# Layers 3 and 4 of a small four-layer model: integer weights and x in two rounded pieces, and a new order on ScalarE

## The reference, cut to what matters

```python
def _dequant(w_int, dtype):            # w_int: int32 from -127 to 127
    return w_int.astype(dtype) * jnp.asarray(1.0 / 127.0, dtype)
gate = jnp.einsum('bsd,hd->bsh', x, wg)      # 128 features -> 384 hidden
up = jnp.einsum('bsd,hd->bsh', x, wu)
h = jax.nn.silu(gate) * up
return jnp.einsum('bsh,dh->bsd', h, wd)

xn = _layernorm(x, axis=-1)            # layer 3: local attention over 5 neighbours
x = x + _L2_attn_ref(xn, ...) + _L2_ffn_ref(xn, w_gate, w_up, w_down)
xn = _layernorm(x, axis=-1)            # layer 4: linear attention with normed heads
x = x + _L3_attn_ref(xn, ...) + _L3_ffn_ref(xn, w_gate, w_up, w_down)
```

## Time and profile before

| | us |
|---|---|
| median of 3 runs (707.17, 710.59, 707.20) | 707.2 |
| the profiled execution's own time | 706.8 |
| its span, first to last instruction | 704.9 |
| TensorE matmul busy in the span | 604.3 (86%) |
| TensorE weight loads | 402.8 (57%) |
| VectorE | 459.6 (65%) |
| ScalarE | 390.2 (55%) |
| GpSimd | 370.7 (53%) |
| mean granted TensorE clock | 0.95 of full |

### The profile page before, as it was taken

How to read it: one execution, slowest core, us unless ns; L and a number is a source line. 1 busy time by engine, 2 the same in 40 slices (tenths; PEclk the granted TensorE clock), 3 DMA queues, 4 the chain that set the end, 5 groups by cost and what they waited for, 6 DMA issues and landing times. The chain is left out here.

```text
span 704.9 us, 9323 instructions
## 1 busy us (share of the span) xinstructions
PE 604.3 (86%) x3100; PEld 402.8 (57%) x3100; DVE 459.6 (65%) x824; ACT 390.2 (55%) x802; POOL 370.7 (53%) x291
## 2 busy tenths in 40 slices
PE   5999888799999988886978698589997888898877
PEld 2433444445454445564667478487887767565546
DVE  6797899999898969754545975133333556445643
ACT  3589899779799744554699352122211237333340
POOL 0688698899899945776101728509014620112220
PEclk9999799999999999997999889689998999999999
DMA  4043333346566401002400114106121100000002
GB/s 117 4 119 57 74 92 103 92 119 128 130 126 127 104 14 54 0 1 76 130 1 2 31 16 139 42 4 167 38 53 37 28 4 1 1 1 0 1 0 60
DMA packets 45817, 40.40 MB, mean 57 GB/s; under 512 B 12183, under 2 KB 32585, under 8 KB 45770
## 3 DMA queue, kind: packets, MB, share of 16 engines
q1 hardware_dynamic: 44746, 37.71, 22.5%
q0 software_dynamic: 1024, 2.10, 1.0%
HBM read 33.70 MB, written 6.09 MB: 56 GB/s over the span
## 5 line engine op out<-in xcount | busy, mean ns | idle before, releaser
L408 PE MATMUL bank<-l0s_ring,all_ident 128*128 128x512 f32 x256 | 120.2, 605 | 4.8 <-POOL l0s_ring L664 4.8
L795 DVE TENSOR_TENSOR_SCAN l0s_ring<-l_XM,l0s_carry,bank 128x512 f32<-128x512 f32 x62 | 74.8, 1257 | 6.3 <-PE bank L391 6.3
L408 PEld LDWEIGHTS bank<-l0s_ring,all_ident 128*128 128x128 f32 x256 | 46.4, 194 | 52.5 <-issue 42.9
L664 POOL TENSOR_TENSOR l0s_ring<-l0s_ring,all_XF 128x1024 f32<-128x1024 f32 x31 | 65.1, 2116 | 10.3 <-DVE l0s_ring L795 9.8
L664 POOL TENSOR_TENSOR l0s_ring<-l0s_ring,l0s_c_rest 128x1024 f32<-128x1024 f32 x32 | 65.4, 2058 | 9.2 <-DVE l0s_ring L795 3.3
L551 ACT ACTIVATE all_XNT<-l_wraw,l_wins 128x256 f32<-128x256 f32 x156 | 66.1, 496 | 0.3 <-PE bank L391 0.2
L391 PEld LDWEIGHTS bank<-all_ident,all_XNT 128*128 128x128 f32 x312 | 36.3, 142 | 34.7 <-issue 26.3
L391 PE MATMUL bank<-all_ident,all_XNT 128*128 128x128 f32 x312 | 42.8, 277 | 10.5 <-DVE l0s_ring L795 7.9
L530 ACT ACTIVATE l_XM<-l_DT,l_negA 128x512 f32<-128x512 f32 x78 | 51.4, 710 | 0.0
L795 DVE TENSOR_TENSOR_SCAN l0s_ring<-bank,l0s_carry,l0s_ring 128x512 f32<-128x512 f32 x34 | 41.5, 1261 | 1.8 <-POOL l0s_ring L654 1.8
L654 POOL TENSOR_TENSOR l0s_ring<-l_DTU,l0s_b_all 128x1024 f32<-128x1024 f32 x20 | 41.0, 2052 | 0.0
(11 more groups left out here) (423 smaller groups left out, 1546.0 us busy)
## 6 DMA issues: line engine op xcount, KB each, us to landing
l0s_c_rest<-bc_rows SPq DMA_DIRECT2D x16, 512.0 KB, 5.4
all_XF<-bc_rows SPq DMA_DIRECT2D x16, 512.0 KB, 5.3
l0s_b_all<-bc_rows SPq DMA_DIRECT2D x20, 256.0 KB, 6.3
l_wall<-in_L_ffn_W SPq DMA_DIRECT2D x14, 256.0 KB, 4.7
all_X<-in_L_attn_x SPq DMA_DIRECT2D x4, 256.0 KB, 3.7
gx<-l1m_TD SPq DMA_DIRECT2D x1, 1024.0 KB, 5.2
gy<-l1m_TD SPq DMA_DIRECT2D x1, 1024.0 KB, 8.6
out<-all_X SPq DMA_DIRECT2D x4, 256.0 KB, 2.3
```

What stands on the lines that cost most here:

```text
L408: last = nc.tensor.matmul(bank_y[j][:, :], S.ident[:, :], hc[n % CRING][:, j, :], start=False, stop=(n % DS == DS - 1))
L664: nc.gpsimd.tensor_tensor(hc[n % CRING][:, :, :], h[n % RING][:, :, :], wide(c_wide[p % HRING][:, n % 2, :]), ALU.mult).then_inc(hc_ready, 1)
L795: nc.vector.tensor_tensor_scan(h[n % RING][:, j, :], factor, added, before, ALU.mult, ALU.add).then_inc(h_ready, 1)
```

## The change

- S.ffn's gate and up weights are stored as F32R (float32r, a 4-byte format that TensorE reads rounded), and hold the integers themselves; the factor 1/127 is applied in silu (scale=QSCALE) and in hidden, which becomes scalar_tensor_tensor.
- x of a block is split in two pieces, xhi (rounded on writing, upper_part, on ScalarE) and xlo = x - xhi (lower_part, on GpSimd, for block 0 on VectorE). gate and up are then two f32r matmuls each, one for each piece, into the same bank.
- upper_part and lower_part have places in the orders of ScalarE, GpSimd and VectorE, and gate_up waits for both pieces.
- silu(3) comes before attend(4) of the local attention; in the loop the first silu of a block comes before heads_squares.
- The four matmuls against the identity in down(b) get is_transpose=True.
- Four weight tiles of layer 4 (wqkv3, bwide, wo3, bow) move into the space of E.w0 (expert 0's weights, used in the stage before).

In the diff, hunks stand in the order GpSimd, TensorE, ScalarE, VectorE. Not shown are lower_part(6) and lower_part(7), which stand behind scale(1) and scale(2) as the others do, and the up's matmuls, which change as the gate's.

```diff
+QSCALE = 1.0 / 127.0
-        ...activation(dst, ..., ACT.Copy, scale=1.0 / 127.0)
+        ...activation(dst, ..., ACT.Copy, scale=1.0 if n % 3 < 2 else QSCALE)
...
-                wqkv3 = ph.sb("wqkv3", [P, 3, P])
-                bwide = ph.sb("bwide", [P, 3 * P])
-                wo3, bow = (ph.sb(n, [P, P]) for n in ("wo3", "bow"))
+                w0 = E.w0[:, :, :].rearrange("p i f -> p (i f)")
+                wqkv3, bwide = w0[:, 0:3 * P].rearrange("p (i d) -> p i d", d=P), w0[:, 3 * P:6 * P]
+                wo3, bow = w0[:, 6 * P:7 * P], w0[:, 7 * P:8 * P]
+                xhi, xlo = ([ph.sb(f"{n}{i}", [P, BLK], F32R) for i in range(2)] for n in ("xhi", "xlo"))
...
+                        def lower_part(b):
+                            pool.wait_ge(xhi_ready, b + 1)
+                            pool.wait_ge(xlo_ready, b)
+                            if b >= 2:
+                                pool.wait_ge(up_done, (b - 1) * HT)
+                            nc.gpsimd.tensor_tensor(xlo[b % 2][:, :], xcols(b), xhi[b % 2][:, :].bitcast(F32), ALU.subtract).then_inc(xlo_ready, 1)
...
                         root(2)
+                        lower_part(1)
                         root(3)
+                        lower_part(2)
+                        lower_part(3)
...
+                        lower_part(NBLK)
                         root(NBLK + 1)
                         add_bias(0)
                         scale(0)
+                        lower_part(NBLK + 1)
                         root(NBLK + 2)
...
...
-                            pe.wait_ge(xf_ready, b + 1)
+                            pe.wait_ge(xhi_ready, b + 1)
+                            pe.wait_ge(xlo_ready, b + 1)
...
-                            nc.tensor.matmul(gate_bank[n][:, :], wguT[:, 0, bass.ts(f, P)], xcols(b), start=True, stop=True).then_inc(gate_done, 1)
+                            nc.tensor.matmul(gate_bank[n][:, :], wguT[:, 0, bass.ts(f, P)], xhi[b % 2][:, :], start=True, stop=False)
+                            nc.tensor.matmul(gate_bank[n][:, :], wguT[:, 0, bass.ts(f, P)], xlo[b % 2][:, :], start=False, stop=True).then_inc(gate_done, 1)
...
-                                    nc.tensor.matmul(out_bank[:, bass.ts(k, P)], S.OUTF[:, bass.ts(t, P)], S.ident[:, :], start=(k == 0), stop=False)
+                                    nc.tensor.matmul(out_bank[:, bass.ts(k, P)], S.OUTF[:, bass.ts(t, P)], S.ident[:, :], start=(k == 0), stop=False, is_transpose=True)
...
+                        def upper_part(b):
+                            act.wait_ge(xf_ready, b + 1)
+                            if b >= 2:
+                                act.wait_ge(up_done, (b - 1) * HT)
+                            nc.scalar.activation(xhi[b % 2][:, :], xcols(b), ACT.Copy).then_inc(xhi_ready, 1)
-                            nc.scalar.activation(sg[n % 2], gate_bank[n][:, :], ACT.Silu).then_inc(silu_done, 1)
+                            nc.scalar.activation(sg[n % 2], gate_bank[n][:, :], ACT.Silu, scale=QSCALE).then_inc(silu_done, 1)
...
+                            if c - 1 in TURN_AT:
+                                upper_part(TURN_AT.index(c - 1))
...
                         values(1)
+                        upper_part(1)
                         copy_x(2)
+                        upper_part(2)
                         for g in range(NG):
                             copy_rows(g)
                             if g + 1 < NG:
                                 exponents(g + 1)
+                            else:
+                                silu(HT)
...
-                        silus(1)
+                        silu(HT + 1)
+                        silu(HT + 2)
+                        upper_part(3)
                         silus(2)
                         for b in range(NBLK):
                             copy_x(NBLK + b)
+                            silu((b + 3) * HT)
                             heads_squares(b)
-                            silus(b + 3)
+                            upper_part(NBLK + b)
+                            silu((b + 3) * HT + 1)
+                            silu((b + 3) * HT + 2)
                             heads_root(b)
...
+                        def lower_part(b):
+                            dve.wait_ge(xhi_ready, b + 1)
+                            nc.vector.tensor_tensor(xlo[b % 2][:, :], xcols(b), xhi[b % 2][:, :].bitcast(F32), ALU.subtract).then_inc(xlo_ready, 1)
-                            nc.vector.tensor_tensor(hid[b % 2][:, f, :], up_bank[n][:, :], sg[n % 2], ALU.mult).then_inc(hid_done, 1)
+                            nc.vector.scalar_tensor_tensor(hid[b % 2][:, f, :], up_bank[n][:, :], QSCALE, sg[n % 2], ALU.mult, ALU.mult).then_inc(hid_done, 1)
...
                                 states(c)
+                            if c - 1 == TURN_AT[0]:
+                                lower_part(0)
...
-        S.ffn = {layer: (ph.sb(f"wguT{layer}", [P, 2, HID]), ...
+        S.ffn = {layer: (ph.sb(f"wguT{layer}", [P, 2, HID], F32R), ...
```

More of the change, by code:

```diff
@@ L7 @@
 BF16 = mybir.dt.bfloat16
+F32R = mybir.dt.float32r
 I32 = mybir.dt.int32
@@ L103, in scalar @@
         dst = wguT[:, n % 3, :] if n % 3 < 2 else wdT[:, :, :].rearrange("p f d -> p (f d)")
-        self.nc.scalar.activation(dst, self.banks[n % len(self.banks)][:, 0:HID], ACT.Copy, scale=1.0 / 127.0).then_inc(self.copied, 1)
+        self.nc.scalar.activation(dst, self.banks[n % len(self.banks)][:, 0:HID], ACT.Copy, scale=1.0 if n % 3 < 2 else QSCALE).then_inc(self.copied, 1)
 DI, DS, DC, DR = 256, 16, 4, 8
@@ L1804, in layer1_phases @@
                                         "normed", "row_turned", "xf_ready"))
+                xhi_ready, xlo_ready = (ph.sem(n) for n in ("xhi_ready", "xlo_ready"))
                 (q_done, k_done, v_done, q_ready, k_ready, v_ready, scored, mx_ready, lowered, ex_ready, tot_ready, rtot_ready, pr_ready,
@@ L1918, in _ @@
                         scale(1)
+                        lower_part(NBLK + 2)
                         root(NBLK + 3)
@@ L1921, in _ @@
                         scale(2)
+                        lower_part(NBLK + 3)
                         add_bias(3)
@@ L2128, in gate_up @@
                                 pe.wait_ge(hid_done, n - 1)
-                            nc.tensor.matmul(up_bank[n][:, :], wguT[:, 1, bass.ts(f, P)], xcols(b), start=True, stop=True).then_inc(up_done, 1)
+                            nc.tensor.matmul(up_bank[n][:, :], wguT[:, 1, bass.ts(f, P)], xhi[b % 2][:, :], start=True, stop=False)
+                            nc.tensor.matmul(up_bank[n][:, :], wguT[:, 1, bass.ts(f, P)], xlo[b % 2][:, :], start=False, stop=True).then_inc(up_done, 1)
                         def down(b, mixed_rows=False):
@@ L2720, in program @@
         S.one_col = S.ones
-        S.ffn = {layer: (ph.sb(f"wguT{layer}", [P, 2, HID]), ph.sb(f"wdT{layer}", [P, HT, P])) for layer in FFN_LAYERS}
+        S.ffn = {layer: (ph.sb(f"wguT{layer}", [P, 2, HID], F32R), ph.sb(f"wdT{layer}", [P, HT, P])) for layer in FFN_LAYERS}
         S.slot = ph.sb("slot", [P, TILES], U32)
```

## The result

| | before | changed |
|---|---|---|
| median of 16 runs of each on one chip, us | 710.53 (706.04 to 714.11) | 701.94 (695.93 to 706.96) |
| profiled execution, its span, us | 706.8, 704.9 | 697.53, 695.8 |
| turn(4) to products(3), profiled, us | 66.4 | 65.1 |

What follows compares the result with a forecast made beforehand. The last stage was taken as bound by TensorE plus a handover with ScalarE (waits for silu). Places A to H sum to -13.05 us, to 693.75; 0.75 added for handovers gives 694.5 us, range 689.5 to 702.

Steps and rivals of the forecast that it cites:

- D: turn(4) to turn(5): the subtraction ahead of root(5) gives back what the matmuls win; 13.7 becomes 13.5 us, -0.2.
- G: turn(7) to products(3), 18.5 us before: gate(18) sooner, products at 9.9 us after it against 12.5; -2.6.
- A: Units 0 to 2 among the chunks (557 to 574 us): gate(0) 0.9 later, cheaper matmuls; -0.8 together.
- B: 598 to 611 us: silu(3) ahead of attend(4), shorter gate(5) and up(5), block 0's turns; -3.4.
- C: gate(6) to turn(4): 5.6 us becomes 4.95, limited by the norm's chain; -0.65.
- H: products(3) to the product with Wo: shorter next unit, gate(23) and up(23); -1.3.
- Part 3: Local output: 16 f32 matmuls against the identity become transposes, 0.45 us in each of four blocks; -1.8.
- E: turn(5) to turn(6): new order removes gate(13)'s wait; 17.9 becomes 15.05 us, -2.85, of it 1.6 the clock.
- F: turn(6) to turn(7): 16.3 becomes 15.05 us, the norm last as in the iteration before; -1.25.
- Rival 2: Clock falls behind waits ahead of turn(5) to turn(7); three or four cost 5 to 6.8 us: 700 to 701; chance 0.11.
- Rival 4: GpSimd and queues: subtractions stretched, or a lower_part waiting for its upper_part; 697 to 703 us; chance 0.09.
- Rivals 1 and 3: An f32r piece costs 0.43 us, total 700.4 (chance 0.14), or 0.86 us, total about 742 (chance 0.04).

Runs made afterwards that it cites:

- before_again: The kernel before, no edit, run and profiled once more; ratio 0.999 (0.995 to 1.002), turn(4) to products(3) 69.5 us, stage 145.0 us.
- after_again: The changed kernel, no edit, run and profiled once more; ratio to the kernel before 0.988, turn(4) to products(3) 65.6 us, stage 136.5 us.
- order_only: The kernel before with the silus' new order alone; ratio to the kernel before 0.978, turn(4) to products(3) 58.7 us, stage 132.7 us.
- turns_only: The kernel before with only the local output's matmuls made transposes (is_transpose=True); ratio to the kernel before 0.993, stage 140.3 us.
- best1: The changed kernel with GpSimd's bias additions behind normalise, roots ahead of scaling and subtraction, root(3) ahead of lower_part(1); ratio to the kernel before 0.972.
- filler: The changed kernel with four never-read matmuls of 384 columns ahead of each of turn(5) to turn(7); ratio to the kernel before 0.984.
- bias_first: The changed kernel with GpSimd's bias additions moved behind the normalise that frees their rows, ahead of the scaling; ratio to the kernel before 0.981.

## Why the prediction was wrong

The mechanism it forecast was there: cheaper units, silus no longer held up by the table load in the loop, and a wait for the norm in the places it named. Two steps failed. It priced normalise behind the root at 1.10 us where it takes 2.05, and it put nothing in the sum for the clock behind the waits of 2.3 us ahead of turn(5) to turn(7), where each wait brought a fall of 1.4 to 1.6 us. They took 5.6 of the 6.9 us forecast for D to G: the clock 4.4, normalise most of the other 1.2.

That the median (701.94) still lies in the range and the profile's span (695.8) between the prediction's own bounds of 688 and 699 speaks for neither: the places of the sum have 5.2 us of 13.05, and the profiled execution owes 3.9 us to what lies ahead of turn(0). A second pair of profiles, before_again and after_again, has 7.7 us from turn(0) on, with three falls in the loop on either side.

- **A**, forecast -0.8. gate(0) came 0.85 later, as forecast. In profiles without other disturbance turn(0) to gate(3) is 42.83 without pieces (order_only, turns_only, before_again) and 42.50 with them: -0.3. The profiled pair has 45.51 and 46.63, +1.1: both were disturbed, the changed one by a normalise(1) of 3.15 us beside two of GpSimd's row additions, which after_again does not show (1.11), and by the fall behind gate(0). What disturbed the other is not known. One half microsecond was a mistake of mine: lower_part(1) stood ahead of root(3), as best1 shows.
- **B**, forecast -3.4, measured -3.3. **C**, -0.65 against -0.55. **H**, -1.3 against -1.2. **Part 3**, -1.8 against -1.8. These hold.
- **D**, forecast -0.2, measured +0.3: the step "normalise(5) 5.8 to 6.9" failed. It took 1.10 from the earlier trace rows, where GpSimd was silent; here add_bias(0), next behind the root that normalise waits for, ran beside it and made it 2.06. The turn came at gate(9) + 7.84 where 7.0 was forecast; gate(9) itself came 0.3 sooner than the sum had it (6.17 behind the turn for 6.5), which hid part of the miss. The Trainium skill, "SBUF — State Buffer", section Who interferes with whom, has VectorE's two-port operations and GpSimd share one port pair, held for a whole instruction while the other blocks. The traces agree in kind: 1.1, 2.05 and 2.84 us with none, one and two neighbours, while the neighbour keeps its 1.27. The lengthening, 0.95 us, is somewhat less than the neighbour's 1.27, and in which mode normalise runs no run here shows.
- **E**, -2.85 against -1.04, and **F**, -1.25 against +0.65. filler has 15.46 and 15.45 where 15.05 was forecast, so 0.4 of the miss in each is normalise, less the cheaper subtraction (0.18) and a first gate that came 0.3 sooner than forecast, and 1.4 to 1.5 is the clock. **G**, -2.6 against -1.2: filler has 15.8 for a forecast of 15.9, so all of the miss is the clock, 1.5.
- The clock therefore failed as a chance, not as a mechanism. Rival 2 named it, with its three places, and it got 0.11; its price of 5 to 6.8 us for three or four falls is near the 4.9 that filler shows for three. That its 700 to 701 lies so near the measured 701.94 is in part chance, for it held neither the long normalise nor what differs ahead of turn(0). The evidence against it was one execution in which "one wait of five" brought a fall. before_again has three. The wait of 2.3 us ahead of each turn, in my own steps D to F, ought to have been priced with a fall behind it.
- The profile of before that I read was light on falls: its stage is 143.1 us, before_again's 145.0. So what removes the waits had more to win than I saw. order_only wins 12.4 us of stage against before_again, with no piece in it, and the whole change gives 1.2% where the order alone gives 2.2%: the pieces, as queued, put back the idle time that the order had removed (waits of 2.85 us ahead of turn(5) to turn(7) where order_only has none, 0.97 and 0.90). How many falls the executions without a profile had is not known.
- Rival 4 (GpSimd's subtractions stretched) looked at the wrong engine: it was VectorE's normalise that was stretched. Rivals 1 and 3 fell with the 0.23 us.

Not settled: why a wait of 1.9 us before a turn cost the clock at turn(5) and turn(7) and not at turn(6) in bias_first, why waits of 2.0 to 2.6 us brought three falls in before_again, one in the first profile of the kernel before and none in turns_only, and why the fall behind gate(5) comes in some executions only (with the same wait of 1.52 us there, in five profiles of eight).

## What to carry to other kernels

When faster matmuls leave the bound to another chain, price what that chain's last steps do once they are last: which instruction of another engine starts with them and lengthens them, and what stands ahead of them in their queue. Price a long wait of TensorE with a stretch at half clock behind it. In the loops of all these profiles each of the nine waits of 2.8 us and more brought one, 8 of 16 waits of 1.9 to 2.6 us did, and no shorter one; most cost 1.4 to 1.6 us. In a queue written by hand the short instruction that others wait for (the root, 1.3 us) goes ahead of the long ones that have slack.

## What was not expected of the hardware

- f32r with a rounded operand costs 0.23 us for 512 columns, against 0.86 for f32 and 0.21 for bf16. The first piece of a block behind an f32 product has a record of 0.69 us in the place of 0.47.
- Matmuls whose product nobody reads can pay: some 2.7 us of them in a gap bought 1.6 us behind it, three times.
- VectorE's normalise doubles beside one instruction of GpSimd (1.10 to 2.05 us), and GpSimd's bias addition keeps its 1.27 us.
- Clock falls differ between executions of one kernel: three waits of 2.0 to 2.6 us in the loop brought one fall in one profile of the kernel before and three in the other.
